# Where and by which queue the second set of inner weights is stored, in a two-level Strassen-Winograd kernel

## What is computed

```python
q_emb = relu(cond @ W3 + b3)                       # (16, 1024)
v_sum = sum(x, axis=1, keepdims=True)
y = relu(((512 * x + v_sum) * q_emb) @ W2 + b2)    # first product, 1024 x 1024 weights
base = y @ W_base + b_base                         # second product, 1024 x 1024 weights
# a router picks 2 of 6 experts of rank 16 for each token; a shared expert of rank 16 is added
out = x + base + (y @ A_s) @ B_s + sum_e gate_e * (y @ A_r[e]) @ B_r[e]
```

## Time and profile before

| | |
|---|---|
| median of 3 runs | 1413.12 us (1412.42 to 1414.57) |
| profiled execution | 1414.27 us, of which the span of the trace is 1412.4 us |
| granted TensorE clock, mean | 0.992 of full |
| PE (TensorE matmul) busy | 1388.9 us, 98% |
| DVE (VectorE) busy | 1037.6 us, 73% |
| ACT (ScalarE) busy | 664.0 us, 47% |
| POOL (GpSimd) busy | 79.5 us, 6% |
| DMA | 255.63 MB, mean 181 GB/s |

### The profile page before, as it was taken

The page is one execution under the profiler, slowest core; times in us unless marked ns, Lnnn a source line. Parts: engine busy times, 40 slices in busy tenths (PEclk is TensorE's granted clock), DMA queues, the critical chain, the costliest instruction groups (busy, mean ns, idle before and its releaser), DMA issues. The chain is left out here.

```text
span 1412.4 us, 18365 instructions
## 1 busy us (share of the span) xinstructions
PE 1388.9 (98%) x6069; PEld 1139.6 (81%) x6069; DVE 1037.6 (73%) x1700; ACT 664.0 (47%) x1209; POOL 79.5 (6%) x170
## 2 busy tenths in 40 slices
PE   9999999999999999999999998699999999999999
PEld 6888888888888888888888886488888888888887
DVE  6976777675776768678879575777777877778665
ACT  7774756556465664746544232333333432244221
POOL 3000100000000000000000001100000000000000
PEclk9999999999999999999999999799999999999999
DMA  8244836445273542528728379638566485756734
GB/s 314 84 156 119 258 123 179 154 126 156 67 204 117 156 140 76 171 96 274 255 73 262 120 235 320 209 107 266 196 233 239 143 274 183 267 181 188 242 119 160
DMA packets 151327, 255.63 MB, mean 181 GB/s; under 512 B 40416, under 2 KB 40672, under 8 KB 151232
## 3 DMA queue, kind: packets, MB, share of 16 engines
q1 hardware_dynamic: 135680, 199.75, 43.5%
q0 software_dynamic: 14688, 53.48, 12.1%
q10 hardware_dynamic: 864, 1.22, 0.2%
HBM read 171.69 MB, written 82.71 MB: 180 GB/s over the span
## 5 line engine op out<-in xcount | busy, mean ns | idle before, releaser
L2760 PE MATMUL ps<-act_hi,w_hi 128*128 128x512 f32 x1504 | 586.5, 390 | 8.5 <-DVE act_lo L1749 8.5
L2761 PE MATMUL ps<-act_lo,w_hi 128*128 128x512 f32 x1504 | 585.6, 389 | 0.0
L2762 PE MATMUL ps<-act_hi,w_lo 128*128 128x512 f32 x1504 | 585.6, 389 | 0.0
L2760 PEld LDWEIGHTS ps<-act_hi,w_hi 128*128 128x128 f32 x1504 | 282.7, 188 | 69.4 <-DVE act_lo L1749 10.1
L2762 PEld LDWEIGHTS ps<-act_hi,w_lo 128*128 128x128 f32 x1504 | 282.7, 188 | 58.7
L2761 PEld LDWEIGHTS ps<-act_lo,w_hi 128*128 128x128 f32 x1504 | 282.8, 188 | 58.5
L1010 ACT ACTIVATE act_hi<-src 128x512 fp32r<-128x512 f32 x208 | 125.0, 622 | 92.2 <-PE ps L2762 91.6
L1749 DVE TENSOR_TENSOR act_lo<-src,act_hi 128x512 fp32r<-128x512 f32 x192 | 129.5, 685 | 21.2 <-ACT act_hi L1010 21.1
L1029 ACT ACTIVATE yhi<-buf 128x512 fp32r<-128x512 f32 x128 | 80.2, 626 | 81.8 <-PE ps L2762 81.4
L1817 DVE SCALAR_TENSOR_TENSOR buf<-ps,bb_sb,buf 128x512 f32<-128x512 f32 x91 | 67.4, 748 | 64.7 <-PE ps L2762 61.0
L2760 PE MATMUL ps<-act_hi,inner_w 128*128 128x512 f32 x252 | 100.4, 398 | 10.7 <-issue 8.7
(11 more groups left out here) (181 smaller groups left out, 1656.6 us busy)
## 6 DMA issues: line engine op xcount, KB each, us to landing
src<-in_xT SPq DMA_DIRECT2D x224, 256.0 KB, 3.6
y_scratch<-buf SPq DMA_DIRECT2D x128, 256.0 KB, 3.0
src<-y_scratch SPq DMA_DIRECT2D x128, 256.0 KB, 5.2
inner_w<-inner_scratch POOLq DMA_DIRECT2D x63, 512.0 KB, 3.8
outT<-buf SPq DMA_DIRECT2D x115, 256.0 KB, 4.5
inner_scratch<-staged POOLq DMA_DIRECT2D x21, 512.0 KB, 4.9
wl_raw<-in_wbase SPq DMA_DIRECT2D x7, 1024.0 KB, 5.7
partner<-y_scratch POOLq DMA_DIRECT2D x12, 512.0 KB, 5.9
```

The lines of the kernel that those rows point to most:

```text
L2760: nc.tensor.matmul(out, wh, a_h, start=start, stop=False, skip_group_check=onto)
L2761: nc.tensor.matmul(out, wh, a_l, start=False, stop=False, skip_group_check=onto)
L2762: return nc.tensor.matmul(out, wl, a_h, start=False, stop=stop, skip_group_check=onto)
```

## The change

The stores of the second set (now `store_four(k)`) are issued by ScalarE on its own DMA queue in place of POOL. They count on two semaphores of their own, `four_stored[0]` and `four_stored[1]`, so weights k = 0 and 1 of this set no longer wait for stores of the set before. Weights 0 to 3 are written, and stored, at other points of ScalarE's program: 0 and 1 after all four high parts of product 6 of pair 1, 2 and 3 after all four high parts of product 0 of pair 2. Weights 4, 5 and 6 are made in pair 2, between the splits of the joined run and inside product 2. On POOL, `load_partner4` moves in all three pairs of pairs from before `stream` of run 1 to just after the load of inner weight 5 in it. The final store of half a tile counts on `buf2_stored` in place of a semaphore of its own.

```diff
             def weights_stored(kind):
                 for q in range(2):
-                    pool.wait_ge(inner_w_stored[q], 16 * ((L2 * (kind + 1) + 1 - q) // 2))
+                    if kind == 2:
+                        pool.wait_ge(four_stored[q], 16 * ((L2 + 1 - q) // 2))
+                    else:
+                        pool.wait_ge(inner_w_stored[q], 16 * ((L2 * (kind + 1) + 1 - q) // 2))
...
             def stream(r):
                 for m in range(2, L2):
                     inner_weights(r, m)
+                    if m == 5 and RUNS[r] in FIRST_OF_TWO:
+                        load_partner4(RUNS[r][0])
...
                 begin(RUN[e, 1])
                 load_partner(e)
-                if e == EARLY:
-                    for c in range(2 * L2, 3 * L2):
-                        store_weights(c)
-                load_partner4(e)
                 stream(RUN[e, 1])
...
(inner_weight_high, on ScalarE)
-                if c >= 2:
+                if c >= 2 * L2:
+                    if k >= 2:
+                        act.wait_ge(four_stored[k % 2], 16 * (k // 2))
+                elif c >= 2:
                     act.wait_ge(inner_w_stored[c % 2], 16 * (c // 2))
...
+            def store_four(k):
+
+                c = 2 * L2 + k
+                act.wait_ge(inner_w_lo, c + 1)
+                act.dma_start(inner_dram[2, INNER_PLACE[k]].bitcast(F32), staged(c).bitcast(F32)).then_inc(four_stored[k % 2], 16)
...
(ScalarE, even: pair 2)
                 if e == EARLY:
-                    inner_weight_high(3 * L2 - 2)
+                    inner_weight_high(2 * L2 + 4)
                 copy_p0(g, 0)
                 lr_high_a(p)
+                if e == EARLY:
+                    store_four(4)
                 inner_high(r, 2)
+                if e == EARLY:
+                    inner_weight_high(2 * L2 + 5)
                 copy_p0(g, 1)
                 copy_p0(g, 2)
                 if e == EARLY:
-                    inner_weight_high(3 * L2 - 1)
+                    store_four(5)
                 for j in range(H):
                     high(g, 2, j)
+                    if e == EARLY and j == 2:
+                        inner_weight_high(2 * L2 + 6)
                 a_max(f)
+                if e == EARLY:
+                    store_four(6)
                 inner_high(r, 3)
...
(ScalarE, pair 1)
                     if g == SECOND - 1 and j in (0, 1):
                         inner_weight_high(L2 + 5 + j)
-                    elif g == SECOND - 1:
-                        inner_weight_high(2 * L2 + j - 2)
+                if g == SECOND - 1:
+                    inner_weight_high(2 * L2)
+                    inner_weight_high(2 * L2 + 1)
+                    store_four(0)
+                    store_four(1)
                 for j in range(H):
                     high(g + 1, 0, j)
-                    if g == SECOND - 1 and j > 0:
-                        inner_weight_high(2 * L2 + 1 + j)
+                if g == SECOND - 1:
+                    inner_weight_high(2 * L2 + 2)
+                    store_four(2)
+                    inner_weight_high(2 * L2 + 3)
+                    store_four(3)
...
(VectorE, even: pair 2)
                 if e == EARLY:
-                    inner_weight_low(3 * L2 - 2)
+                    inner_weight_low(2 * L2 + 4)
                 lr_low_a(p)
                 add_p0(r, 0)
                 inner_low(r, 2)
                 inner_t3(r)
+                if e == EARLY:
+                    inner_weight_low(2 * L2 + 5)
                 add_p0(r, 1)
                 for j in range(H):
                     t2(g, j)
-                if e == EARLY:
-                    inner_weight_low(3 * L2 - 1)
                 for j in range(H):
                     low(g, 2, j)
+                    if e == EARLY and j == 2:
+                        inner_weight_low(2 * L2 + 6)
...
(VectorE, before_next)
                     if g == SECOND - 1 and j == 1:
                         inner_weight_low(2 * L2 + 2)
                         inner_weight_sums(2)
-                    elif g == SECOND - 1 and j > 1:
-                        inner_weight_low(2 * L2 + 1 + j)
+                    elif g == SECOND - 1 and j == 2:
+                        inner_weight_low(2 * L2 + 3)
```

More of the change, by code:

```diff
@@ L272, in adaln_ffn @@
         x21_added = sem("x21_added")
-        last_half_stored = sem("last_half_stored")
         inner_hi_done = sem("inner_hi_done")
@@ L286, in adaln_ffn @@
         c12_base = sem("c12_base")
+        four_stored = [sem(f"four_stored{r}") for r in range(2)]
         a_ready = sem("a_ready")
@@ L307, in adaln_ffn @@
         RUN = {key: r_of for r_of, key in enumerate(RUNS)}
+        FIRST_OF_TWO = tuple((e_of, 1) for e_of, n_of in RUNS if n_of == 4)
         START = []
@@ L799, in _ @@
             sp.dma_start(outT[2 * LAST, K - 1, :, 0:T // 2], buf2[:, H - 1, 0:T // 2]).then_inc(buf2_stored[H - 1], 16)
-            sp.wait_ge(last_half_stored, 16)
             for j in range(H):
                 sp.wait_ge(buf1_stored[j], 16 * 2 * ALL)
-                sp.wait_ge(buf2_stored[j], 16 * ALL)
+                sp.wait_ge(buf2_stored[j], 16 * (ALL + (j == H - 1)))
                 sp.wait_ge(buf3_stored[j], 16 * ALL)
@@ L1685, in _ @@
             act.wait_ge(c21_done, four(ALL - 1, H - 1) + 1)
-            act.dma_start(outT[2 * LAST, K - 1, :, T // 2:T], buf2[:, H - 1, T // 2:T]).then_inc(last_half_stored, 16)
+            act.dma_start(outT[2 * LAST, K - 1, :, T // 2:T], buf2[:, H - 1, T // 2:T]).then_inc(buf2_stored[H - 1], 16)
         @block.vector
```

## The result

| | before | after |
|---|---|---|
| median | 1413.84 us (1412.42 to 1414.86, 4 runs) | 1388.55 us (1387.62 to 1389.98, 4 runs) |
| profiled execution, span | 1414.27, 1412.4 us | 1388.26, 1386.5 us |
| granted TensorE clock, mean | 0.992 | 1.0 |

The ratio is 0.9823, with a 95% interval of 0.9806 to 0.984. The gain is 25.3 us by the medians; 25.3 was forecast, and the time came out 0.75 us above the forecast of 1387.8.

What follows compares the result with a forecast made beforehand. TensorE bounds the kernel, busy 98% of the span, except for stalls around the start of pair 2. Ceiling 26.4 - 1.0 (stall left) - 0.1 = 25.3 us gain, so 1413.12 - 25.3 = 1387.8 us, range 1386 to 1396.5.

Steps and rivals of the forecast that it cites:

- The ceiling: Most that the change could gain: 25.92 us in pair 2 plus 0.46 us at 864, 26.4 us.
- The ruler: First matmul of product 0 to issue of inner weight 4: pair 4 20.86 us, pair 2 46.78, difference 25.92.
- The second stall: TensorE's 8.68 us wait before inner 2 of pair 2, inner weight loads late on POOL; goes, with one clock fall.
- The fourth rival: Inner 2 waited for something other than its weights, so 8.7 + 3.6 us stay: 1400; chance 0.11 with the second.
- The first stall: Waits of 7.2, 0.8 and 2.0 us up to inner 0 of pair 2, through ScalarE's weight writes waiting for stores.
- Weight 6 of the first set: On ScalarE before weights 0 and 1; claimed to keep its place in time, 859.10 in the trace of before.
- The landing of store 0: Time for store 0 of the second set to land from ScalarE: 6.0 us taken, bounds 3.5 and 9.3.
- The stall of 1.0 us before inner 0: Wait of TensorE left in pair 2: low part ready at 879.4, needed at 878.4; 0.4 us with landing 5.3 or less.
- The 0.46 us at 864: TensorE idle before pair 2; removed because tile 3's low part of product 6 comes about 0.9 us earlier.
- Weight 6 in product 2: Tight place in pair 2: inner 3's low part ends at E + 4.8, needed at E + 5.4; costs nothing.
- The second and third rivals: Second: an old stall returns in pair 2, 1400.1, 0.11 with the fourth rival; third: ladder of landings, slower than before, 0.04.
- The first rival: Store 0 lands late (9.3 us): 4.4 us stall before inner 0, one clock fall of 3.6, 1394.7 us; chance 0.23.

Runs made afterwards that it cites:

- in the second: The kernel after run once more with no edit, for the spread between executions: 1389.82 us, ratio 0.9835.

## Why the prediction held, point by point

- **The ceiling.** The ruler's 25.92 us became 25.90. Pair 4 was a sound measure of pair 2 without stalls, the clock and PE's refilling included.
- **The second stall, 8.68 us and one fall of the clock, 12.3 us.** Shown by itself at 11.7 by the medians and 12.2 by the spans. It comes back when the partner load is put first, with all stores on ScalarE, and stays away with all stores on POOL. So the cause is the order in POOL's program, and not, as the prediction's heading "Stores off POOL" has it, that the stores were there. The fourth rival falls.
- **The first stall, store 0 "behind two inner weight loads and two partner loads".** That was only part of it. POOL reached those loads at 868.19, after 6.78 us of waiting for the first set's last store, and issuing four of them then took 2.5 us. The experiment that puts stores 0 and 1 back there gives the same picture, with 7.1 us from POOL's program and 1.2 from the longer landing. The forecast needed only that store 0 leaves about 863, so this did it no harm.
- **Weight 6 of the first set "stays where it is".** It did not: its high part was written between 856.40 and 859.32 in eight profiles of kernels in the new order that show it, and the kernels in the old order show 856.02 and 858.59 beside the 859.10 of the prediction. One profile of before was read as a fixed time. It is set by the landings of stores one after the other (the last of them took 5.2 us to weight 6 in one profile and 7.1 in another), and it spreads by about 3 us whatever the kernel. This gave the kernel after 2.6 us of lead in its first profile (store 0 at 860.40, forecast 863.0) and 1.0 in the second.
- **The landing of store 0, 6.0 us.** Measured 6.4, 7.2, 6.8 and 6.2 from ScalarE, 7.9 from POOL. The value was low by up to 1.2 us on ScalarE, within its bounds, and the earlier issue made up for it. Weight 2 was written at 866.78 and 869.21, forecast 869.0, and far from the 872 that would have refuted it.
- **The stall of 1.0 us before inner 0.** 0 in the first profile and 0.91 in the second, with the releaser that was named. In the second, where weight 2 came when it was forecast (869.21 for 869.0), the path took what was worked out: inner 0 could start at 879.80, for 879.4. The slope of 1 us per us holds over the eight profiles. The 0.4 us that a landing of 5.3 us or less would leave were counted with store 0 at 863.0. In the first profile all of this came up to 2.6 us sooner, and VectorE had time over: it was idle for 1.02 us before the last `c21` ahead of inner 0, waiting for TensorE. With weight 2 early enough there is no wait at all. Whether VectorE's work would have left 0.4 us from 863.0 on no run shows.
- **The 0.46 us at 864.** Gone, and worth more: a matmul after it stands at 871.98 now and 872.08 before, although the kernel after was 0.67 us behind at 820, ahead of anything that the change touches. 0.77 us came back. Of it 0.62 was the delay of the matmul that waited (864.45, where 863.60 + 0.227 was due), and the rest the slower matmuls behind it.
- **Issue on ScalarE, 0.45 us, or 1.3 at worst.** In the kernel after it was 0.33 to 0.37 even in the full stretch. The worst case exists too: where a store was issued less than 1 us behind another, in other runs, it took 0.5 to 1.31 us (1.31 for store 1 with weights 0 and 1 made sooner). One by itself, in the kernel after:

```profile
868.17 0.36 ACTq L1203 DMA_DIRECT2D inner_scratch<-staged  x1
```

- **Weight 6 in product 2.** Group 3 of product 0 ends at E = 893.75, and VectorE's timeline gives inner 3's low part:

```profile
897.00 1.21 DVE L2187 TENSOR_TENSOR act_lo<-buf,act_hi 128x1024 fp32r<-128x1024 f32 x1
```

  It ends at 898.21, E + 4.46, where 4.8 was worked out and 5.4 allowed. The second and third rivals fall with it: no ladder of landings showed on TensorE in pair 2.
- **`load_partner4` later, nothing.** Its user comes 913.62 - 902.48 = 11.14 us after the issue of inner weight 5, as in the working (11.15), and doesn't wait; in pairs 4 and 6 VectorE's list of waits has no DMA of `partner` either. In pair 2:

```profile
913.62 1.22 DVE L2121 SCALAR_TENSOR_TENSOR partner<-partner,src 128x1024 f32<-128x1024 f32 x1
```

- **Inner weight 2** was issued 882.09 - 876.06 = 6.03 us after product 0 began, where 5.6 was written. In pair 4 of before the same step took 5.92, so 5.6 was a slip; nothing hung on it.
- **The first rival, priced at 1394.7.** Made by hand, it gave 1393.3 and 1394. The stall was 3.3 us where 4.4 was priced with weight 2 at the same time, and the fall of the clock 1.7, where 3.6 was carried over from stalls of 7 to 9 us.
- **What the prediction did not price.** The two partner loads before inner 0 landed in 7.3 and 8.7 us before, and in 11.9 and 13.8 us in the kernel after, which has stores 0 and 1 in flight there. VectorE waited 0.70 us for one of them, and TensorE nothing (the last lines of this document show it).
- **The sum.** 25.90 + 0.77 - 0.67 = 26.0 us against 26.01 between the two profiled executions. The median forecast was 0.75 us low, for reasons that partly cancel: the median of before was taken 1.15 us below the profile and that of after lies 0.3 above, which is 1.45 low; no stall and the larger gain at 864, less the 0.67 of the start, put the profiled execution 0.7 us below its forecast of 1389.0.

## What to carry to other kernels

When TensorE waits for "issue", read the timeline of the queue that loads its operand, and look for an instruction that waits for something else ahead of the load; put the loads that are needed first there, and look at what the queue's own earlier instructions wait for; in this kernel it then did not matter which engine issued the rest. A stretch of the same program without the stall, in another iteration, gives the ceiling of the gain, clock included. A time in one profile that is set by a DMA's landing is not fixed: take several executions before a margin of 1 us is built on it.

## What the runs showed of the hardware

- With the DMA share above 1 (1.06 to 1.10 at 855 to 860), the same store of the first set landed after 5.2 to 7.1 us in eleven profiles, seen from the weight that waited for it. With the landings before it, the time of that weight spread by about 3 us (856.02 to 859.32), while the runs of the kernel after stayed within 0.2% of each other (1387.62 to 1389.98).
- Behind 2 MB of loads on its queue such a store took 9.1 us, with none ahead 5.8 to 7.9 (5.8 where weights 0 and 1 were made sooner, 7.9 from POOL behind another store). Extra copies of 512 KB ahead of it on its queue cost 1.5 to 2.7 us each.
- Waits of 0.57, 0.91 and 1.18 us brought no fall of the clock; 0.96 and 2.29 us, with three matmuls between them, did, and it cost 1.7 us. After waits of 7 to 9 us a fall, with the refilling, had cost 3.6, and after one of 13.58 us 2.8. The price of a fall is not one number.
- In the kernel after, VectorE waited in pair 2 for a load of `partner` (that of `load_partner`, issued at 866.90) and for a store of `outT` (brackets), which the prediction had not foreseen and which cost TensorE nothing:

```profile
878.92 1.23 DVE L2121 SCALAR_TENSOR_TENSOR partner<-partner,src 128x1024 f32<-128x1024 f32 x1 [0.70 <-DMA partner<-y_scratch]
...
882.96 1.22 DVE L2145 SCALAR_TENSOR_TENSOR buf<-partner 128x1024 f32<-128x1024 f32 x1 [1.68 <-DMA outT<-buf]
```
